# Second norm's rows of batches 0 to 9 read back from DRAM by quarters and transposed in 32x32 blocks on the vector engine; their gate runs two batches behind

## The reference

```python
x = x + tanh(g_xattn) * attention(layernorm(x), ctx)      # one head: q = n@Wq, k,v = ctx@Wkv
n2 = layernorm(x)                                          # "second norm"
logits = n2 @ gate_w + gate_b                              # 8 experts
probs = softmax(logits, axis=tokens)                       # over the 256 tokens of a batch
vals, idx = top_k(probs, 2)                                # each token picks two experts
# three relu layers 512x512 per expert on the tokens sent to it,
# then per expert: v[e] = sum over tokens of y * weight
x = x + tanh(g_ffn) * sum of v[e] over the token's two experts
```

## Time and profile before

| | |
|---|---|
| median of 3 runs | 930.74 us (929.98 to 931.37) |
| the profiled execution | 929.86 us, of it 928.1 us from the first to the last instruction |
| PE busy | 909.5 us, 98% of the span |
| DVE, ACT, POOL busy | 694.9, 503.5, 276.2 us |
| one batch of the first stage | 19.95 us, batch after batch |
| granted TensorE clock, whole span | 0.988 of full speed |

### The profile page before, as it was taken

One profiled execution on the slowest core, in us unless ns is written; L12 is line 12 of the kernel. 1 busy time (PEld: TensorE's weight loads), 2 busy tenths in 40 slices (PEclk: granted clock), 3 DMA queues, 4 the chain that ended last, 5 costly groups with the idle time before them and its releaser, 6 DMA issues.

```text
span 928.1 us, 18701 instructions
## 1 busy us (share of the span) xinstructions
PE 909.5 (98%) x5746; PEld 858.4 (92%) x5746; DVE 694.9 (75%) x1305; ACT 503.5 (54%) x707; POOL 276.2 (30%) x314
## 2 busy tenths in 40 slices
PE   8999999999999999999999999999999999999985
PEld 6989988888988888999999999999999999999981
DVE  6667767777767877967777777777777777777756
ACT  5355444455444368556666666666666666666521
POOL 4224454444444557742111111111111111110003
PEclk9999999999999999999999999999999999999995
DMA  7423332223232355457766888853753753752009
GB/s 239 159 105 124 104 124 91 91 91 136 95 108 69 88 158 122 133 145 211 187 197 167 247 251 245 247 177 109 185 170 111 192 167 111 191 169 64 18 16 362
DMA packets 91924, 138.67 MB, mean 149 GB/s; under 512 B 28528, under 2 KB 56944, under 8 KB 88688
## 3 DMA queue, kind: packets, MB, share of 16 engines
q1 hardware_dynamic: 84464, 120.86, 42.4%
q0 software_dynamic: 7424, 17.38, 7.2%
HBM read 106.66 MB, written 31.53 MB: 149 GB/s over the span
## 4 chain that ended last, share of the span: by engine, by line
PE 91%; DVE 3%; issue 1%; POOL 1%; DMA 1%; SPq 1%; ACT 1%; DVEq 0%; POOLq 0%; ACTq 0%
PE bank L1339 28%; PE bank L1341 28%; PE bank L1340 28%; DVE x_all L1329 2%; PE bank L1353 1%; PE bank L1422 1%; PE bank L1463 1%; PE bank L1465 1%; DMA idx<-slot_pair 0%; POOL slot_pair L633 0%; DMA wk_raw<-in_wk_t 0%; PE bank L1373 0%; PE bank L1479 0%; PE bank L1606 0%; PE bank L1414 0%
## 5 line engine op out<-in xcount | busy, mean ns | idle before, releaser
L1339 PE MATMUL bank<-h_hi,w_hi 128*128 128x352 f32 x744 | 241.4, 324 | 0.0
L1341 PE MATMUL bank<-h_hi,w_lo 128*128 128x352 f32 x744 | 240.1, 323 | 0.0
L1340 PE MATMUL bank<-h_lo,w_hi 128*128 128x352 f32 x744 | 239.0, 321 | 0.0
L663 POOL DMA_INDIRECT xg<-xn_dram,idx x72 | 93.0, 1291 | 359.3 <-DMA idx<-slot_pair 343.6
L952 DVE TENSOR_TENSOR w_lo<-w_raw,w_hi 128x2048 fp32r<-128x2048 f32 (+1 forms) x74 | 166.5, 2250 | 23.8 <-ACT w_hi L824 18.7
L841 ACT ACTIVATE h<-bank,bias 128x352 f32<-128x352 f32 x192 | 95.8, 551 | 139.8 <-PE bank L1341 114.6
L824 ACT ACTIVATE w_hi<-w_raw 128x2048 fp32r<-128x2048 f32 x71 | 135.5, 1908 | 35.5 <-PE bank L1341 33.1
L952 DVE TENSOR_TENSOR h_lo<-h,h_hi 128x704 fp32r<-128x704 f32 x88 | 78.1, 888 | 83.9 <-ACT h_hi L847 83.9
L1339 PEld LDWEIGHTS bank<-h_hi,w_hi 128*128 128x128 f32 x744 | 139.8, 188 | 0.1
L1340 PEld LDWEIGHTS bank<-h_lo,w_hi 128*128 128x128 f32 x744 | 139.8, 188 | 0.0
L1341 PEld LDWEIGHTS bank<-h_hi,w_lo 128*128 128x128 f32 x744 | 139.3, 187 | 0.0
(11 more groups left out here) (218 smaller groups left out, 1721.4 us busy)
## 6 DMA issues: line engine op xcount, KB each, us to landing
w_raw<-in_w SPq DMA_DIRECT2D x24, 1024.0 KB, 5.4
xq<-rows_dram SPq DMA_DIRECT2D x80, 176.0 KB
w_raw<-in_w SPq DMA_DIRECT2D x48, 256.0 KB
rows_dram<-xg SPq DMA_DIRECT2D x20, 512.0 KB, 3.3
wb<-slot_pair SPq DMA_DIRECT2D x24, 352.0 KB
xt_raw<-in_x_t SPq DMA_DIRECT2D x16, 512.0 KB, 3.9
c_raw<-in_ctx_t SPq DMA_DIRECT2D x16, 512.0 KB
x_all<-in_x SPq DMA_DIRECT2D x16, 512.0 KB
```

What stands on the lines that cost most here:

```text
L663: pool.indirect_dma_start(xg[0:n, c], None, rows, bass.IndirectOffsetOnAxis(ap=idx[0:n, c, 0:1], axis=0)).then_inc(gathered, 16)
L1339: pe.matmul(out_ap, lh, rh, start=(i == 0), stop=False)
L1340: pe.matmul(out_ap, lh, rl, start=False, stop=False)
L1341: last = pe.matmul(out_ap, ll, rh, start=False, stop=(i == n - 1))
```

## The change

Three things change together. First, `GATE_BLOCKS = 10`: for batches 0 to 9 PE no longer transposes `xn2`. SP reads the rows that `store_xn2` has just written back from `xn2_dram` in four transfers, each a quarter of the features onto 32 partitions (`load_gate_rows`), and one DVE instruction over 128x1024 elements transposes 32x32 blocks into `gt_raw` (`gate_blocks`, inside `attended` of the next batch). ACT and DVE split it from there (`gt_high_late`, `gt_low_late`, one instruction each in place of two).

Second, for batches 0 to 10 the gate runs two batches behind (`late`): in `batch(b)` PE's order is `scores(b)`, `values(b)`, `gate_logits(b-2)`, `pt_transposes(b)`, `x_times_a(b+1)`, `gate_transposes(b-2)`, the first half of `p_times_v(b)`, `ranks(b-2)`, the second half. On DVE `two_best(b-2)` now stands between the halves of `qa_low(b+1)` and `slots(b-2)` behind them, ahead of `attended(b)`. Batch 11 makes the passage, and 12 to 15 keep the order from before.

Third, what follows from it: the remaining transposes of PE read every fourth feature, to give the order of features that the blocks give; the gate's weights are loaded to match, in four transfers in place of one; the loop covers batches 3 to 10, and 11 to 14 are unrolled.

```diff
-BATCHES = (-1, 3, B - 3, B - 1)
+BATCHES = (-1, 3, 11, B - 1)
...
+GATE_BLOCKS = 10
+LATE_GATE = GATE_BLOCKS + 1
...
+def by_dve(m):
+    return not isinstance(m, int) or 0 <= m < GATE_BLOCKS
+def late(m):
+    return not isinstance(m, int) or 0 <= m < LATE_GATE
+def in_time(m):
+    return isinstance(m, int) and LATE_GATE <= m < B
+def by_pe(m):
+    return isinstance(m, int) and GATE_BLOCKS <= m < B
...
-            alloc(ph, "experts_own_room", [P, EXPERTS_OWN // 4 - NSLOT // P], F32)
+            alloc(ph, "xg_room", [P, TH * D - NSLOT // P], F32)
+            gate_rows = alloc(ph, "gate_rows", [P, S // QB, P], F32)
+            gt_raw = alloc(ph, "gt_raw", [P, DC, S], F32)
+            alloc(ph, "experts_own_room", [P, EXPERTS_OWN // 4 - TH * D - S // QB * P - DC * S], F32)
...
+        gate_rows_in, gt_ready = sem("gate_rows_in"), sem("gt_ready")
...
-            sp.dma_start(gw_raw[:], gate_w).then_inc(s_small, 16)
+            for q in range(NQ):
+                sp.dma_start(gw_raw[q * QB:(q + 1) * QB], gate_w[:, q].rearrange("(i k) e -> i k e", k=DC)).then_inc(s_small, 16)
...
+            def load_gate_rows(m):
+                need(sp, xn2_out, 16 * (m + 1))
+                need(sp, gt_ready, m)
+                for q in range(NQ):
+                    rows = xn2_dram[bass.ds(m * S, S), q * P:(q + 1) * P].rearrange("(g b) d -> b g d", b=QB)
+                    sp.dma_start(gate_rows[q * QB:(q + 1) * QB], rows).then_inc(gate_rows_in, 16)
             def batch(b, parity):
...
+                if by_dve(b - 1):
+                    load_gate_rows(b - 1)
...
+            def gt_high_late(m):
+                need(act, gate_done, m)
+                act.wait_ge(gt_ready, m + 1)
+                act.activation(gt_hi[:], gt_raw[:], ACT.Copy).then_inc(gt_his, 2)
             def gt_high(m):
...
-                    need(act, tg_done, 2 * m + k + 1)
+                    need(act, tg_done, 2 * (m - GATE_BLOCKS) + k + 1)
...
             def norm2(m):
...
-                need(act, tg_done, 2 * m)
+                if by_pe(m - 1):
+                    need(act, tg_done, 2 * (m - GATE_BLOCKS))
...
             def batch(b, parity):
+                if by_dve(b - 2):
+                    gt_high_late(b - 2)
...
+                if late(b - 2):
+                    gate_low(b - 2)
+                    pt_high(b)
...
-                if exists(b, B):
+                if exists(b, B) and not late(b - 2):
...
-                if exists(b - 1, B):
+                if by_pe(b - 1):
...
+                if late(b - 2):
+                    gate_exp(b - 2)
...
-                if exists(b - 1, B):
+                if in_time(b - 1) and not late(b - 2):
...
+                if in_time(b - 1) and late(b - 2):
+                    gate_low(b - 1)
+                    gate_exp(b - 1)
...
-            act.wait_ge(s_small, 64)
+            act.wait_ge(s_small, 16 * (3 + NQ))
...
-            def v_pt_low(m):
+            def v_low(m):
...
+            def pt_low(m):
...
+            def gate_blocks(m):
+                dve.wait_ge(gate_rows_in, 16 * NQ * (m + 1))
+                need(dve, gt_his, 2 * m)
+                dve.transpose(gt_raw[:].rearrange("p k (g b) -> p g k b", b=QB),
+                              gate_rows[:].rearrange("p g (i k) -> p g k i", k=DC)).then_inc(gt_ready, 1)
+            def gt_low_late(m):
+                dve.wait_ge(gt_his, 2 * (m + 1))
+                dve.tensor_tensor(gt_lo[:], gt_raw[:], gt_hi[:].bitcast(F32), ALU.subtract).then_inc(gt_los, 2)
             def gt_low(m):
...
-            def qa_low(m):
+            def qa_low(m, halves=range(2)):
...
-                for k in range(2):
+                for k in halves:
...
             def gate_softmax(m):
+                gate_maximum(m)
+                gate_scale(m)
+            def gate_maximum(m):
...
+            def gate_scale(m):
...
+                if by_dve(m - 1):
+                    gate_blocks(m - 1)
...
             def batch(b, parity):
...
-                if exists(b - 2, B):
+                if in_time(b - 2) and b - 2 > LATE_GATE:
...
+                if by_dve(b - 2):
+                    gt_low_late(b - 2)
...
+                if isinstance(b, int) and b - 2 == LATE_GATE:
+                    two_best(b - 2)
...
-                    v_pt_low(b)
-                if exists(b - 1, B):
+                    v_low(b)
+                if late(b - 2):
+                    gate_maximum(b - 2)
+                if exists(b, B):
+                    pt_low(b)
+                if by_pe(b - 1):
...
-                if exists(b - 2, B):
+                if in_time(b - 2):
...
-                if exists(b + 1, B):
+                if late(b - 2):
+                    gate_scale(b - 2)
+                    qa_low(b + 1, [0])
+                    two_best(b - 2)
+                    qa_low(b + 1, [1])
+                    slots(b - 2, parity)
+                elif exists(b + 1, B):
...
-                if exists(b - 1, B):
+                if in_time(b - 1) and not late(b - 2):
...
+                if in_time(b - 1) and late(b - 2):
+                    gate_softmax(b - 1)
...
-            v_pt_low(B - 1)
+            v_low(B - 1)
+            pt_low(B - 1)
...
-                                            src[:, c, dc * P:(dc + 1) * P], ident[:])
+                                            src[:, c, dc::DC], ident[:])
...
-            def x_times_a(m):
+            def x_times_a(m, between=None):
...
+                    if n == DC - 1 and between is not None:
+                        between()
...
-            def p_times_v(m):
+            def p_times_v(m, between=None):
...
+                    if c == RC - 1 and between is not None:
+                        between()
...
             def gate_transposes(m):
...
-                    last = pe.transpose(R_PROB[:, c * E:(c + 1) * E], probs[:, c * P:(c + 1) * P],
-                                        ident[0:E, 0:E])
+                    rows = slice(c, None, RC) if by_dve(m) else slice(c * P, (c + 1) * P)
+                    last = pe.transpose(R_PROB[:, c * E:(c + 1) * E], probs[:, rows], ident[0:E, 0:E])
...
             def batch(b, parity):
...
-                if exists(b - 2, B):
+                if in_time(b - 2) and b - 2 > LATE_GATE:
...
-                if exists(b - 2, B):
-                    ranks(b - 2)
+                if in_time(b - 2):
+                    if b - 2 == LATE_GATE:
+                        gate_transposes(b - 2)
+                    else:
+                        ranks(b - 2)
+                if late(b - 2):
+                    gate_logits(b - 2)
...
-                if exists(b - 1, B):
+                if by_pe(b - 1):
...
+                if isinstance(b, int) and b - 2 == LATE_GATE:
+                    ranks(b - 2)
...
+                if late(b - 2):
+                    gate_transposes(b - 2)
...
-                if exists(b - 1, B):
+                if in_time(b - 1) and not late(b - 2):
...
-                    p_times_v(b)
+                    p_times_v(b, (lambda: ranks(b - 2)) if late(b - 2) else None)
+                if in_time(b - 1) and late(b - 2):
+                    gate_logits(b - 1)
```

## The result

The changed kernel takes 936.01 us, median of 4 runs (935.88 to 936.17), where the kernel before took 930.68 in the same session (929.98 to 931.37): a ratio of 1.0059 [1.0047, 1.0071]. It is slower by 5.3 us, and the forecast was 6.45 us faster. The profiled execution took 935.88 us with a span of 934.1, at a mean granted clock of 0.986 (0.988 before).

What follows compares the result with a forecast made beforehand. PE's gapless first-stage stream, 19.95 us a batch, was taken as the bound. -8.2 + 0.1 + 0.65 + 0.55 + 0.45 = -6.45 us took 930.74 to 924.3 us; own range 922.3 to 926.5, overall range 921.8 to 928.0.

Steps and rivals of the forecast that it cites:

- Does DVE keep up?: DVE's turn in each batch: operands reach PE in time, slacks 0.4 to 0.6 us, none at ranks; waits 0.55 and 0.45.
- the contention rule: DVE instructions with two SBUF inputs and GpSimd ones reading SBUF block each other for the whole instruction; no row showed it.
- The pair that was named: gt_low_late on DVE beside norm2_scale on POOL: gt_low_late could start 0.72 us late, 0.3 past its slack.
- the +2.9 us of that rule: Possible added time if POOL's norm2_scale delays DVE's gt_low_late in nine turns; not in the forecast sum.
- PE's stream: First stage on PE: without its eight transposes, 0.82 us saved in each of batches 2 to 10, together 8.2 us.
- The block transpose: DVE's added instruction over 1024 elements in each turn: 2.0 us by size, bounds 1.2 and 2.75.
- The round trip: Storing the norm's rows to DRAM and reloading them in four loads, 4.8 us: hidden by at least 2 us.
- DVE's turn as bound: Rival: slow block transposes or POOL holding gt_low_late make nine turns 0.3 us longer, run 927.0; chance 0.16.
- 0.55 and 0.45: Waits of PE for DVE: 0.05 us at ranks in 11 batches, and 0.05 per turn in nine turns.
- The strided transposes: PE's 48 transposes of batches 10 to 15 reading every fourth feature: 0.014 us more each, 0.65 us in all.
- The passage: Return to the old order behind the loop: ranks in the middle lose 0.05 us each in batches 11 and 12.
- No gain arrives: Rival: PE's 6 us come back as a wait in the first expert tiles, run 930.7; chance 0.05.

Runs made afterwards that it cites:

- e1: Changed kernel, but ACT writes the gate's exponentials over the logits in PSUM and DVE scales them from there into probs: 926.78 us.
- e7: e1, and DVE writes probs in the order PE reads them, in one piece instead of every second element: 925.44 us.
- e3: Changed kernel, but in batches with a late gate POOL does norm2_scale(b) ahead of the scatters, send_pairs(b-2): 943.65 us.
- e5: Kernel before, with all 128 gate transposes on PE reading every fourth feature and the gate's weights loaded in four transfers: 930.75 us.
- e4: Changed kernel with the late gate order kept, but PE does all transposes of xn2, with no block transposes or quarter loads: 940.65 us.
- e2: Changed kernel, but in batches with a late gate ACT does gate_exp(b-2) ahead of context_high(b+1): 930.21 us.
- e8: e7 with GATE_BLOCKS = 12 in place of 10 and the loop over batches 3 to 12: 924.31 us.
- e9: e4, and POOL does norm2_scale(b) ahead of the scatters, send_pairs(b-2), in batches with a late gate: 932.91 us.

## Why the prediction was wrong

**The step that failed is "Does DVE keep up?", together with the contention rule.** The layout starts DVE's turn at `gate_transposes`, at 15.6, and takes for granted that PE starts them there. It gives what DVE must do after them, with slacks of 0.4 to 0.6, and then "some 1.5 us to spare before the next `gate_transposes`". What `gate_transposes` itself waits for was never laid out: the gate's exponentials, their scaling on DVE, and `c_lo` on POOL at the same time. The rule that decides was in the prediction, but weighed for one pair, `gt_low_late` with `norm2_scale`. Every pair of a DVE instruction and a POOL one that the new order brings together had to be gone through. The numbers for it were there: `c_lo` takes 2.41 us in the kernel before, and the text itself put `context_low` "near 15", 0.6 ahead of `gate_transposes` at 15.6. So was a case of it, though the prediction says that its rows have none. In batch 15 of the kernel before, outside those rows, the scaling lies under a subtraction of POOL, takes 1.33 and ends 0.16 after it, and PE waits for it:

```profile
362.36 3.36 POOL L673 TENSOR_TENSOR h_lo<-h,h_hi 128x704 fp32r<-128x704 f32 x2
...
364.55 1.33 DVE L1033 TENSOR_SCALAR probs<-gexp,gsum 8x256 f32<-8x256 f32 x1
...
366.03 0.26 PE L1479 MATMUL bank<-ident,probs 8*128 8x8 f32 x2 [0.49 <-DVE probs L1033]
```

**The pair that was named held the other engine.** `gt_lo` did meet `norm2_scale`, and it was POOL that was held (0.91 and 1.02), not DVE, so the +2.9 us of that rule did not come; e1 has the same overlap and runs at 926.78. What it does is to make ACT's `xn`, and so `probs`, late; whether the changed kernel would have waited without that stays open, as said at e1. The prediction takes the block "for the whole instruction" from the Trainium skill; the section says these words of the two-port modes; of two SBUF inputs it says that the engines contend, and it calls contention in general an exclusive lock. The trace shows it for this kind too: POOL's steps end at 168.72 and 169.83, 0.08 and 0.05 after `gt_lo` and `xt_lo`.

**PE's stream: right.** A gain of 0.82 a batch was forecast. With hold and stride gone (e7) the eight intervals of the loop sum to 154.18, 0.68 a batch less than before; the forecast with its waits was 153.8. Ranks cost 0.35 and 0.11, as said. Not foreseen: `gate_transposes` read `probs` with a stride, 0.11 us a batch in ten batches, 926.78 - 925.44 = 1.3 us by the medians and 0.9 by the intervals up to batch 11.

**The block transpose: right.** The tile's own view, of the changed kernel, minimum, median and maximum in ns, with the loads that feed it; it answers to the earlier trace rows:

```profile
L1043 DVE STREAM_TRANSPOSE gt_raw<-gate_rows x10: 2012/2032/2075, 60.0 to 244.3; 128x1024 f32<-128x1024 f32 x10
...
DMA to landing us min/median/max: 2.4/2.7/3.4
```

2.03 us for 2.0 forecast.

**The round trip: right, with room to spare.** SP issues the four loads at 154.12 in 1.85 (1.86 forecast) and they land 2.5 to 2.9 later (2.7 in the median of all batches), where 4.8 was taken for the four. That is near 158.7, and the block transpose starts at 162.52. No wait of DVE on these rows in the whole trace. e3 shows where that cover ends: with scatters beside them the loads land after 5.3 and DVE waits in five batches.

**DVE's turn as bound: no.** Between 100 and 260 us the weight load of `ranks` waits 0.4 at most and PE itself isn't listed for it; `gate_logits`, `values` and `x_times_a` don't wait for DVE. 0.55 and 0.45 were allowed for it.

**The strided transposes: a little less.** 0.09 for eight (e5) is 0.011 each, so 0.54 for 48, and 0.65 was taken.

**The passage: too cheap.** From batch 11 to 14, e7 takes 62.58, 2.73 more than before; from batch 11 to 15 1.91 more, where some 0.6 was forecast. Part is the gate's work pushed back from the first batches; part is a wait of 0.9 for `xn` at PE's first transposes behind the loop, the one of e4. From batch 14 to the first block transpose of the experts e7 takes 109.52, the kernel before 109.21 and e5, which has the old order, 109.90. PE's wait of 2.4 before batch 15's transposes, for `et_lo`, is in e5 as well. So nothing here shows the rival "No gain arrives". The last stretch, behind the last block transpose, differs by 0.9 between kernels with the same code there (71.3 to 72.3); that stays open.

**Two slips in the sums.** The low end of the forecast's own range, no waits and the strided reads free, is 924.3 - 0.55 - 0.45 - 0.65 = 922.65 and not 922.3. And `ranks` in the middle cost 0.46 - 0.36 = 0.10 more in each of batches 11 and 12 by the prediction's own rows, where it takes 0.05. Neither changes the outcome.

Added up: e7's 925.44 is 1.1 us from the forecast of 924.3. The working of PE's gain stood; 9.2 us of hold and 1.3 of stride were missing from it. That the rest is as small as 1.1 us is partly luck: the first intervals came out 0.9 better than forecast, and the passage 1.3 worse.

## What to carry to other kernels

When an order is changed on one engine, write down which pairs of DVE and POOL instructions it makes overlap, and price each as if the one that starts second ended only when the other does: a 0.34 us step on PE's path took 1.9 here. The cure was cheap: read one operand from PSUM, or cut the long instruction in two. And ask of every step on the critical engine what its own operand hangs on, the ones that moved relative to their producers first.

## What the runs showed of the hardware

- A `tensor_scalar` of 8x256 fp32 from SBUF to SBUF: 0.34 us alone, 1.92 beside POOL's 2.39 us subtraction, 2.51 where it meets its start (e3). From PSUM to SBUF under the same subtraction: 0.47.
- A comparison of two 128x32 tiles in SBUF: 0.19 alone, 0.29 to 1.81 under `c_lo` (e2, e3).
- POOL's steps on 128x2 elements take 0.19 to 0.72 alone and up to 1.81 (e8) beside DVE's subtractions of SBUF tiles; the step that takes 0.20 alone takes 1.02.
- With POOL's scatters issued just before them, SP's loads of the gate's rows land after 5.3 us and not 2.7, those of `xt_raw` after 5.5 to 6.2 and not 3.9 (e3, e9).
- Weights of PE read at every second fp32 element: 0.11 us more for two loads.
